# Edge sort of a GNN and FFN stack: two records underway instead of one, and a bucket table laid out lane by lane

## What is computed

```python
edge_index = jnp.stack([src, dst])
x = x + _L0_gnn_ref(_layernorm(x), edge_index, ...)
x = x + _L0_ffn_ref(_layernorm(x)[None], ...)[0]
x = x + _L1_gnn_ref(_layernorm(x), edge_index, node_vec1, ...)   # 4 attention blocks
x = x + _L1_ffn_ref(_layernorm(x)[None], ...)[0]                 # 16 experts, top 2
x = x + _L2_gnn_ref(_layernorm(x), edge_index, edge_type_8, edge_weight, ...)
x = x + _L2_ffn_ref(_layernorm(x)[None], ...)[0]
x = x + _L3_gnn_ref(...)
x = x + _L3_ffn_ref(...)[0]
```

```python
e = jax.nn.leaky_relu(e_src + e_dst, NEG_SLOPE)
e = e * (1.0 + et_emb[edge_type])
e = e * edge_weight[:, None]
e_max = jnp.zeros((n, h_), x.dtype).at[dst].max(e)
e = jnp.exp(e - e_max[dst])
e_sum = jnp.zeros((n, h_), x.dtype).at[dst].add(e)
out = jnp.zeros((n, h_, d_), x.dtype).at[dst].add(msg)
```

## Time and profile before

| | us |
|---|---|
| median of 3 runs | 1818.19 |
| the three runs | 1817.63, 1818.19, 1823.83 |
| the profiled execution, its own time | 1826.41 |
| its span, first to last instruction | 1824.3 |
| TensorE busy in the span | 1594.4 (87%) |
| VectorE busy | 898.4 (49%) |
| GpSimd busy | 642.5 (35%) |
| mean granted TensorE clock | 0.928 |

### The profile page before, as it was taken

One profiled execution on the slowest core, in us unless ns is written; L12 is line 12 of the kernel. 1 busy time (PEld: TensorE's weight loads), 2 busy tenths in 40 slices (PEclk: granted clock), 3 DMA queues, 4 the chain that ended last, 5 costly groups with the idle time before them and its releaser, 6 DMA issues.

```text
span 1824.3 us, 23037 instructions
## 1 busy us (share of the span) xinstructions
PE 1594.4 (87%) x7110; PEld 880.6 (48%) x7111; DVE 898.4 (49%) x2199; ACT 501.0 (27%) x1607; POOL 642.5 (35%) x748
## 2 busy tenths in 40 slices
PE   6989999998697999999993496679699899999698
PEld 3534444446354546464551373524244455555455
DVE  8878888887634443433433035978722101011322
ACT  1134444446422414232230112411210211111233
POOL 5867787772332322223233812537500000000000
PEclk9999999998798999999996697579899999999899
DMA  7030101006323142222212572566515222210020
GB/s 308 4 103 24 58 24 58 24 7 169 84 71 125 53 90 78 79 84 56 86 37 87 131 250 79 163 149 186 162 69 190 69 75 69 98 58 23 10 60 18
DMA packets 132572, 162.75 MB, mean 89 GB/s; under 512 B 62041, under 2 KB 74601, under 8 KB 132114
## 3 DMA queue, kind: packets, MB, share of 16 engines
q1 hardware_dynamic: 105888, 116.45, 20.6%
q0 software_dynamic: 18752, 29.91, 6.2%
q10 hardware_dynamic: 7858, 15.44, 2.5%
HBM read 145.87 MB, written 15.88 MB: 89 GB/s over the span
## 4 chain that ended last, share of the span: by engine, by line
PE 69%; DMA 14%; DVE 11%; issue 3%; ACT 2%; POOL 1%; DVEq 0%; ACTq 0%; POOLq 0%
PE psum L377 68%; DMA tab_sorted<-rec,pos 12%; DVE arena L2586 2%; DVE stats L468 1%; DVE ring L1277 1%; PE psum L1008 1%; PE psum L2245 0%; POOL arena L624 0%; DMA arena<-tab_x 0%; DMA tab_x<-xn,gate 0%; POOL tab_x L2288 0%; ACT arena L2837 0%; DMA x<-in_x 0%; DVE xn L2038 0%; DVE mv L469 0%
## 5 line engine op out<-in xcount | busy, mean ns | idle before, releaser
L377 PE MATMUL psum<-arena 128*128 128x24 bf16 (+8 forms) x2026 | 325.8, 319 | 30.8 <-DVE arena L654 12.8
L377 PE MATMUL psum<-arena,ring 128*128 (+1 forms) x1504 | 325.4, 363 | 9.3 <-issue 6.2
L377 PE MATMUL psum<-xT,ring 128*128 128x384 f32 x928 | 319.4, 506 | 10.1 <-ACT ring L3020 4.2
L377 PEld LDWEIGHTS psum<-arena 128*128 128x128 bf16 (+5 forms) x2026 | 199.3, 149 | 163.5 <-issue 74.7
L377 PE MATMUL psum<-ring,arena 128*128 128x512 f32 (+1 forms) x592 | 271.1, 605 | 7.3 <-ACT arena L2837 3.8
L377 PE MATMUL psum<-ring,xT 128*128 128x512 f32 x552 | 252.3, 609 | 2.9 <-DMA bc<-in_wide 1.8
L377 PEld LDWEIGHTS psum<-xT,ring 128*128 128x128 f32 x928 | 182.4, 198 | 140.6 <-issue 30.0
L377 PEld LDWEIGHTS psum<-arena,ring 128*128 128x128 bf16 (+1 forms) x1504 | 139.2, 115 | 130.3 <-issue 28.9
L2128 POOL DMA_INDIRECT tab_sorted<-rec,pos x104 | 99.9, 961 | 242.6 <-DMA tab_sorted<-rec,pos 226.0
L1059 ACT ACTIVATE ring<-ring 128x128 f32<-128x128 f32 x416 | 123.3, 297 | 173.3 <-DVE ring L1343 173.3
L377 PEld LDWEIGHTS psum<-ring,arena 128*128 128x128 f32 (+1 forms) x592 | 102.6, 187 | 133.7 <-issue 132.6
(11 more groups left out here) (456 smaller groups left out, 1635.4 us busy)
## 6 DMA issues: line engine op xcount, KB each, us to landing
ring<-in_L_ffn_w SPq DMA_DIRECT2D x22, 1024.0 KB, 8.3
ring<-in_L_gnn_m_w SPq DMA_DIRECT2D x8, 1024.0 KB, 6.1
ring<-in_L_ffn_expert_weights SPq DMA_DIRECT2D x8, 1024.0 KB, 5.4
ring<-tab_key ACTq DMA_DIRECT2D x24, 256.0 KB, 3.2
ring<-in_L_gnn_Wv SPq DMA_DIRECT2D x5, 1024.0 KB, 5.1
tab_w<-xn SPq DMA_DIRECT2D x6, 768.0 KB, 14.4
ring<-in_L_gnn_Ww SPq DMA_DIRECT2D x4, 1024.0 KB, 17.1
ring<-in_L_gnn_wq SPq DMA_DIRECT2D x4, 1024.0 KB, 6.3
```

Source lines behind the costliest of these rows:

```text
L377: return nc.tensor.matmul(o, a, b, start=start, stop=stop)
```

## The change

Three edits, in the kernel's own words:
- A third value of `most`, `OF_RECORDS = 2`, takes the place of `BEHIND_LOOP = 1` in the second scatter alone. The 76 late records of the first scatter keep theirs.
- The index `pos` of the first scatter is no longer `tmp_e` itself but `r_f * 104 + q_f`: edge place `128 q + r` goes to row `104 r + q` of `tab_bucketed`. It is now worked out behind `r_f`.
- The read back takes `(r q) k -> r q k` instead of `(q r) k -> r q k`, so `rec` gets the same contents from a table in which the rows of a lane lie together.

```diff
-        IN_FRONT, BEHIND_LOOP = 2, 1
+        IN_FRONT, BEHIND_LOOP, OF_RECORDS = 2, 1, 2
...
             od.link(V.tensor_reduce(tmp_e, before9.rearrange("p k t -> p t k"), AX, ALU.add))
-            V.tensor_copy(pos[:], tmp_e).then_inc(pos_ready, 1)
             od.link(V.tensor_scalar(q_f, tmp_e, 1.0 / P, -63.5 / P, ALU.mult, ALU.add))
             od.link(V.tensor_scalar(q_f, q_f, ROUND, None, ALU.add))
             V.tensor_scalar(q_f, q_f, -ROUND, None, ALU.add).then_inc(slot_ready, 1)
             dve.wait_ge(slot_ready, 1)
             od.link(V.scalar_tensor_tensor(out=r_f, in0=q_f, scalar=-float(P), in1=tmp_e, op0=ALU.mult, op1=ALU.add))
+            V.scalar_tensor_tensor(out=pos[:], in0=r_f, scalar=float(ST), in1=q_f, op0=ALU.mult, op1=ALU.add).then_inc(pos_ready, 1)
...
-            nc.gpsimd.dma_start(rec[:], tab_bucketed.rearrange("(q r) k -> r q k", r=P)).then_inc(bucketed_loaded, 16)
+            nc.gpsimd.dma_start(rec[:], tab_bucketed.rearrange("(r q) k -> r q k", r=P)).then_inc(bucketed_loaded, 16)
...
-                few_underway(pool, q, RECORDS, BEHIND_LOOP)
+                few_underway(pool, q, RECORDS, OF_RECORDS)
```

## The result

| | before | changed |
|---|---|---|
| median of the runs, us | 1821.01 (4 runs) | 1790.56 (4 runs) |
| lowest to highest | 1817.63 to 1825.9 | 1787.03 to 1793.01 |
| profiled execution, its span | 1824.3 | 1787.1 |
| ratio, with its 95% interval | | 0.983 (0.980 to 0.986) |

The changed kernel is faster by 1.7%, 30.5 us between these medians. The profiled pair differs by more, 37.2 us of span.

A forecast was written before the change was run, and what follows sets the result against it. TensorE's 47.0 us wait for dispatched rows was taken as the bound, with GpSimd late behind the second scatter. The dispatch's 32.4 us gain, other terms zero, gave 1818.19 - 32.4 = 1785.8 us, range 1778 to 1798.

The forecast's parts named there:

- What bounds: At the dispatch, GpSimd is 32.5 us late behind the second scatter's last record; the most a faster sort can give.
- The dispatch's rest: After the dispatch's six issues, landing 4.82 us and load 4.88 unchanged; TensorE starts at 996.7 instead of 1029.11.
- The pace: Second scatter with two records underway: 1.65 us a step instead of 3.20, last record started at 839.
- The read back: Ahead of the second scatter: 3.3 us instead of 16.0 landing; alone worth 13 us, with the other edit nothing more.
- The index: VectorE's work on `pos`: at most +0.3, at least -0.12 us on the key sort's start; taken as zero.
- Rows scattered further apart: First scatter's first 20 records, rows now 1,664 bytes apart: between -1 and +3 us; taken as zero.
- Rival A: GpSimd's DMAs worked off one after another, pace stays 3.20 us a step: gain 13 us, time 1805; chance 0.06.
- Rival B: Two records' short-row writes into `tab_sorted` stretch each other's landings; at 8 us, time near 1898; chance 0.03.
- Rival C: TensorE's clock falls less in a shorter wait: at most 4 us more, time 1782; chance within the full gain's 0.88.
- From the profile to the median: The profile's 32.4 us taken off the median; were its 8.2 us excess all in delaying records, time 1794.0.

The follow-up runs named there:

- the kernel with the loads beside the dispatch: The changed kernel with SP waiting for the first experts' places before loading the sorted table, so both loads go out beside the dispatch: 1791.12 us in a single run.
- the repeat: The changed kernel itself, run again beside the kernel before on the same chip: 1789.87 us, ratio 0.984 (0.981 to 0.988).
- the new table alone: The changed kernel with one record of the second scatter underway again and the new table layout kept: 1808.23 us, ratio 0.994 to the kernel before.
- the dispatch-first one: The kernel before, one record underway and old table, with the second scatter's last 13 records behind the six dispatch DMAs: 1811.5 us, ratio 0.997.
- the kernel with 104 records again: The changed kernel with all 104 records of the second scatter sent a second time, same rows to same places: 1848.87 us, ratio 1.018 to the kernel before.

## Why the prediction was right

The forecast was a median of 1785.8 us with a range of 1778 to 1798; 1790.56 was measured. The kernel before is at 1821.01 with a fourth run where the forecast started from 1818.19, which is 2.8 of the 4.8 us; the gain itself was put at 32.4 and is 30.5. Point by point:

- **What bounds.** Right. The price was the difference between the places being ready and GpSimd being free, not the scatter's share of the chain. The dispatch's first start moved by 32.0 us (32.4 forecast for the last one; it too moved by 32.0). GpSimd reached it 0.76 us after the cast's end, where I had allowed 0.1.
- **The dispatch's rest.** The landing was taken as unchanged, with up to 1.5 us of possible gain. It gave 2.1 (4.82 to 2.70), for the reason named and not counted, as the kernel with the loads beside the dispatch showed. TensorE's start came 34.1 us earlier against 32.4, which is the 32.0 and this 2.1.
- **The pace.** 1.92 us a step against the 1.65 taken and bounds of 1.26 and 3.20. The first 20 records of the other scatter were a kinder stretch. The last record started at 864.4 and not at 839; of the 140 us to spare some 115 were left, so it entered nothing.
- **The read back.** 2.8 us of landing against 3.0 in the like-shaped row; start of the scatter at 667.1 against 669.3. Its worth alone, put at 13 us, was 11.5 by the medians and 17.2 in the profile's wait.
- **The index.** The operation behind `r_f` is 0.31 us long, and the one-hot work behind it starts at 23.83 instead of 23.51, at the upper bound of 0.3. Little of it gets further: GpSimd's first record starts at 81.09 instead of 81.01. Zero, as taken, to within 0.1 us.

```profile
23.03 0.31 DVE L1221 SCALAR_TENSOR_TENSOR pos<-xT 128x96 int32<-128x96 f32 x1
```

- **Rows scattered further apart.** No price: the 20 early records go from 81.09 to 111.81, 1.62 us a step where it was 1.65.

```profile
81.09 1.20 POOL L840 DMA_INDIRECT tab_bucketed<-rec,pos  x1 [0.18 <-issue]
...
111.81 0.96 POOL L840 DMA_INDIRECT tab_bucketed<-rec,pos  x1 [0.30 <-issue]
```

- **Rival A**, one at a time in spite of two: out, by starts 1.26 apart and by the kernel with seven underway. **Rival B**, writes in each other's way: out. Two records of short rows into the sorted table land in 2.1 us at the median, as one did. **Rival C**, the clock: out. It was still low when work resumed, and rose as late after it as before the change. In steps of 2 us from TensorE's start at L2245 the granted clock was 0.50 up to 8 us in both kernels, 0.71 before and 0.78 now from 8 to 10, and 1.00 behind that. The stretches of the changed kernel:

```profile
985.00:997.00 12.00, 1.99 (x10) 2.00 (x11) 0.16 (x1) 0.91 (x2) 10.84 (x10) 0.50 0.60 218
1001.00:1005.00 4.00, 4.00 (x26) 4.00 (x25) 0.00 (x0) 2.14 (x5) 3.75 (x4) 0.64 0.00 0
1005.00:1009.00 4.00, 4.00 (x27) 2.96 (x26) 0.69 (x1) 0.37 (x2) 3.75 (x4) 1.00 0.86 225
```

- **From the profile to the median.** The weakest step. In profiles the span fell by 37.2 us, 34.1 of it by TensorE's start and 3.1 behind it: from that start to the end the changed kernel took 792.1 us (1787.1 - 995.01) and 795.2 before (1824.3 - 1029.11). The 3.1 are not the change's: in the changed kernel's second profile this part took 794.1 us (1786.8 - 992.68). By the medians the gain was 30.5 here and 29.8 in the repeat, less than the 32.4 of the sum and than the 34.1 of the profiles. The text had named what could do it: the profile's 8.2 us over the median may lie in the records, so that the late end of the scatter is a matter of the run. In favour: the kernel before spreads over 16 and 17 us in its sets of 21 and 17 runs, and the new table alone over 13 in ten, while the changed kernel spreads over 6 in four and 6 in five, and the dispatch-first one over 4 in twelve. Against it: the kernel before spreads over only 4.6 us in its set of seven, the kernel with 104 records again, whose wait is the longest, over 6.7 in four, and the profile nearest to a median run has the full wait. So the cause of these few us is open.
- **Two slips that change nothing.** Where the text puts the unprofiled wait at 24.2 us, 24.2 (32.4 - 8.2) is the gain; the wait would be 38.8. And 1794.0 with the spread of 5.6 above gives 1799.6 as the upper end, not 1798.

## What to carry to other kernels

Price a long stretch of waiting on one engine by what the others wait for at its end, here 32 us of 330, and then find how much of a faster version only becomes slack: by the prediction's sum 3.01 us a step would have done where two underway give 1.92, and seven records underway brought nothing over two. An engine that works in order carries its lateness into whatever stands behind it, so either the work ahead becomes shorter or the urgent instructions move ahead of it. The second looks cheaper than it is: behind the moved instructions everything that waits for the delayed work (here the tiles behind SP's wait, for TensorE and for VectorE, and the gathers behind `edge_factors`) has a deadline of its own, and each must be priced by the slack in front of it.

## What the runs showed of the hardware

- Indirect DMAs of 128 rows of 16 bytes, issued by GpSimd, overlap well: 3.20 us a step with one underway, 1.92 with two, 1.27 with up to seven, while the median landing goes from 2.1 to 2.1 to 3.2 us. Seven left 0.3 us of waiting in all, beside weight tiles of 1 MB.
- The shape of a DMA's rows costs the engine that issues it as well as the transfer, here on GpSimd: the same 208 KB took GpSimd 4.16 us and landed in 16.0 as 13,312 pieces of 16 bytes, and took 0.59 and 2.8 us as 128 pieces of 1,664.
